# Pre-norm attention and FP8 linear layer on one core: transposed scores follow the plain ones at 16 steps in place of 32

## What is computed

```python
def reference(L0_attn_x, ...):                   # x: (16, 512, 256), fp32; 16 heads of 16
    ...
        qkv = jnp.einsum('bsd,ed->bse', x, qkv_w) + qkv_b
        ...
        scores = jnp.einsum('bhqe,bhke->bhqk', q, k) * scale
        attn = jax.nn.softmax(scores, axis=-1)
        out = jnp.einsum('bhqk,bhke->bhqe', attn, v)
        ...
        out = jnp.einsum('bsd,ed->bse', out, proj_w) + proj_b
    ...
        x_q = jnp.clip(x / input_scale, -FP8_MAX, FP8_MAX)
        x_dq = x_q.astype(jnp.float8_e4m3fn).astype(x.dtype) * input_scale
        out = jnp.einsum('bsi,oi->bso', x_dq, w_dq) + bias
    ...
    x = x + _L0_attn_ref(_layernorm(x, axis=-1), ...)
    x = x + _L0_ffn_ref(_layernorm(x, axis=-1), ...)
```

## Time and profile before

| what | value |
|---|---|
| three runs | 1053.39, 1055.44, 1057.67 us (median 1055.44) |
| profiled execution | 1050.12 us, span 1048.3 us |
| PE, DVE, ACT, POOL busy | 90%, 80%, 63%, 50% of the span |
| mean granted clock of TensorE | 0.954 |
| DMA | 79.4 MB, 50.5% of 16 engines |

### The profile page before, as it was taken

One profiled execution on the slowest core, in us unless ns is written; L12 is line 12 of the kernel. 1 busy time (PEld: TensorE's weight loads), 2 busy tenths in 40 slices (PEclk: granted clock), 3 DMA queues, 4 the chain that ended last, 5 costly groups with the idle time before them and its releaser, 6 DMA issues.

```text
span 1048.3 us, 16257 instructions
## 1 busy us (share of the span) xinstructions
PE 945.9 (90%) x5796; PEld 443.0 (42%) x5796; DVE 843.0 (80%) x1186; ACT 655.7 (63%) x1209; POOL 522.7 (50%) x533
## 2 busy tenths in 40 slices
PE   3476989999999999999999999999999999999884
PEld 2243334444444434454444444444444444433333
DVE  3586788888888989888888889888888888896226
ACT  3013776767676676767676676767676776766560
POOL 3141344828284654728293755638282846524242
PEclk9675999999999999999999999999999999999795
DMA  4928092656638192746648291836556380911010
GB/s 138 116 44 94 26 119 41 97 88 77 108 45 139 21 115 51 108 77 82 103 56 129 30 117 39 119 66 92 93 68 96 40 125 14 117 35 42 2 41 20
DMA packets 44289, 79.40 MB, mean 76 GB/s; under 512 B 9904, under 2 KB 13104, under 8 KB 44208
## 3 DMA queue, kind: packets, MB, share of 16 engines
q1 hardware_dynamic: 44208, 78.36, 50.5%
HBM read 18.42 MB, written 8.39 MB: 26 GB/s over the span
## 4 chain that ended last, share of the span: by engine, by line
PE 81%; ACT 6%; POOL 4%; DVE 3%; issue 2%; DMA 2%; SPq 1%; ACTq 0%; POOLq 0%; DVEq 0%
PE ps_t L457 28%; PE ps_o L489 23%; PE ps_m L371 9%; PE ps_s L471 5%; ACT pt L568 5%; PE ps_m L382 5%; PE ps_m L408 5%; PE ps_m L439 3%; POOL xnT_p L907 2%; SPq L282 1%; ACT xnT L587 1%; POOL xnT_p L905 1%; DVE mx L686 1%; DMA ks<-parts 1%; PE ps_m L355 1%
## 5 line engine op out<-in xcount | busy, mean ns | idle before, releaser
L568 ACT ACTIVATE pt<-ps_t 128x512 f32<-128x512 f32 x1024 | 557.5, 599 | 242.5 <-PE ps_t L457 238.0
L686 DVE TENSOR_REDUCE mx<-ps_s 128x2 f32<-128x1024 f32 x512 | 617.6, 1213 | 93.3 <-PE ps_s L471 87.9
L457 PE MATMUL ps_t<-qs,ks 50*128 50x512 f32 x1024 | 406.9, 467 | 41.1 <-ACT pt L568 34.7
L471 PE MATMUL ps_s<-ks,qs 48*128 48x512 f32 x1024 | 399.8, 472 | 20.0 <-DMA ks<-parts 11.4
L457 PEld LDWEIGHTS ps_t<-qs,ks 50*128 50x128 f32 x1024 | 164.7, 187 | 360.2 <-ACT pt L568 288.4
L489 PE MATMUL ps_o<-pt,vt 128*32 128x512 f32 x2048 | 275.3, 610 | 0.2 <-ACT pt L568 0.2
L471 PEld LDWEIGHTS ps_s<-ks,qs 48*128 48x128 f32 x1024 | 160.1, 189 | 31.3 <-DVE mx L686 16.1
L905 POOL CAST xnT_p<-xnT 128x512 fp32r<-128x512 f32 x30 | 18.3, 611 | 195.2 <-ACT xnT L587 195.2
L371 PE MATMUL ps_m<-xnT_p,wqkv_p 128*128 128x512 f32 x360 | 101.1, 417 | 7.6 <-POOL xnT_p L907 7.6
L939 POOL TENSOR_TENSOR on<-ot,rden 128x256 f32<-128x256 f32 x63 | 39.6, 628 | 103.8 <-DVE rden L745 103.8
L930 POOL TENSOR_TENSOR parts<-parts 128x512 f32<-128x512 f32 x60 | 81.2, 1353 | 4.9
(11 more groups left out here) (94 smaller groups left out, 766.4 us busy)
## 6 DMA issues: line engine op xcount, KB each, us to landing
qs<-parts SPq DMA_DIRECT2D x192, 128.0 KB, 6.5
ks<-parts SPq DMA_DIRECT2D x192, 128.0 KB, 7.0
xin<-in_x SPq DMA_DIRECT2D x16, 512.0 KB, 4.6
xres<-in_x SPq DMA_DIRECT2D x16, 512.0 KB, 5.9
out<-h SPq DMA_DIRECT2D x15, 512.0 KB, 9.0
qs<-nmax SPq DMA_DIRECT2D x128, 8.0 KB, 5.7
pt<-in_qkv_wT SPq DMA_DIRECT2D x1, 768.0 KB, 6.5
out<-h SPq DMA_DIRECT2D x2, 256.0 KB, 2.0
```

The lines of the kernel that those rows point to most:

```text
L457: nc.tensor.matmul(ps_t[:, g, :], ks[par][rows, slot, keys], qs[par][rows, slot, :], start=True, stop=True).then_inc(st_done, 1)
L471: done = nc.tensor.matmul(ps_s[:, s % 2, g, :], qs[par][rows, slot, queries], ks[par][rows, slot, :], start=True, stop=True)
L568: nc.scalar.activation(pt[n % 2][:, w % 2 + 2 * a, w // 2, :], ps_t[:, a, :], ACT.Exp, scale=SCALE).then_inc(exp_done, 1)
L686: dve.tensor_reduce(mx[:, t, :, s % (STEPS // 2)], ps_s[:, s % 2, :, :], AX_X, ALU.max).then_inc(max_done, 1)
```

## The change

The transposed scores of a batch now begin at step 16 of the slot that has its plain scores, and end at step 15 of the next one, not at steps 0 and 31 of the next one. For this the maxima go in four quarters of 8 steps: four transposes, four splits and 16 row transfers of 4 KB a batch where there were two, two and 8 of 8 KB. The stacks are sent in four groups of 6 transfers (q and k parts apart) where there were two of 12, and a batch's result in two halves. The heads of a quarter must be those whose plain scores are done, so the order of heads changes, with the rows of the projection weights. All steps of the side work are placed anew, and the orders on DVE, POOL and SP with them. The output projection is done in slot u = b + 2 and half of a batch's v projection in slot b.

```diff
-PROJECT_V = (4, 6)
-PROJECT_OUT = (8, 10)
-TRANSPOSE_X = (12, 14)
-PROJECT_QK = (16, 18, 20, 22)
-TRANSPOSE_MAX = (25, 5)
-TRANSPOSE_HQ = 26
-LINEAR = (28, 30)
-OUT_BLOCKS = (11, 19, 27, 3)
-OUT_BACK = (22, 5)
-COPY_OT = (24, 6)
...
+HALF_STEPS = STEPS // 2
+QUARTER = STEPS // 4
+NQ = 4
+
+PROJECT_V = (30, 0)
+TRANSPOSE_X = (2, 4)
+PROJECT_QK = (6, 12, 20, 22)
+TRANSPOSE_HQ = 10
+LINEAR = (14, 18)
+PROJECT_OUT = (26, 28)
+TRANSPOSE_MAX = (8, 16, 24, 1)
+OUT_BLOCKS = (27, 3, 11, 19)
+OUT_BACK = (6, 21)
+COPY_OT = (8, 23)
...
# SP, slot
             def slot(u, par, present):
                 if present(2):
-                    rows(u - 2, par, 1)
+                    rows(u - 2, par, 3)
                 if present(-2):
                     load(u + 2, par)
+                if present(1):
+                    rows(u - 1, 1 - par, 0)
                 if present(0):
                     stack(u, par, 0)
-                if present(1):
-                    rows(u - 1, 1 - par, 0)
                 if present(2):
                     reload(u - 2, par)
+                if present(3):
+                    store(u - 3, 0)
+                if present(1):
+                    rows(u - 1, 1 - par, 1)
                 if present(0):
                     stack(u, par, 1)
                 if present(3):
-                    store(u - 3, 1 - par)
+                    store(u - 3, 1)
+                if present(0):
+                    stack(u, par, 2)
+                if present(1):
+                    rows(u - 1, 1 - par, 2)
+                if present(0):
+                    stack(u, par, 3)
...
# PE, slot
                 for s in range(STEPS):
-                    if present(2):
-                        scores_t(u - 2, par, s, 0)
+                    bt, st = (u - 2, s + HALF_STEPS) if s < HALF_STEPS else (u - 1, s - HALF_STEPS)
+                    if 0 <= bt < B:
+                        scores_t(bt, bt % 2, st, 0)
...
# POOL, slot
             def slot(u, par, present):
-                later = not isinstance(u, int) or u > 0
-                if present(0):
-                    layernorm_x(u, par)
-                if present(3):
-                    out_divide(u - 3, 3)
-                    low_oT(u - 3, 1)
-                if present(0) and later:
+                if present(2):
+                    out_divide(u - 2, 1)
+                if present(0) and u > 0:
                     low_xnT(u, 0)
-                if present(2):
-                    out_divide(u - 2, 0)
-                if present(0) and later:
                     low_xnT(u, 1)
                 if present(3):
-                    layernorm_h(u - 3)
-                if present(0) and later:
+                    round_fp8(u - 3)
+                if present(0) and u > 0:
                     split(u, 0)
...
```

More of the change, by code:

```diff
@@ L156, in block_kernel @@
         stacked = [[sem(f"stacked{t}{i}") for i in range(2)] for t in range(NT)]
-        rows_in = [sem(f"rows_in{t}") for t in range(NT)]
-        stored = sem("stored")
+        rows_in = [sem(f"rows_in{r}") for r in range(NQ)]
+        stored = [sem(f"stored{i}") for i in range(2)]
         met = sem("met")
@@ L220, in present @@
             def present(u):
-                return lambda behind: 0 <= u - behind < B
+                return lambda behind, ends=B: 0 <= u - behind < ends
             for u in range(NSLOT - 1):
@@ L276, in stack, with rows @@
                 settled()
-                for r, (pq, pk) in enumerate(zip(Q_PARTS, K_PARTS)):
+                dst, picks = (qs, Q_PARTS) if n % 2 == 0 else (ks, K_PARTS)
+                for r, part in enumerate(picks):
                     for g in range(2):
                         rows = slice(HALF * g + HD * r, HALF * g + HD * (r + 1))
[L280 to L286, removed]
+                        sp.dma_start(dst[par][rows, NS * t:NS * (t + 1), :].bitcast(F32),
+                                     parts[HALF * g:HALF * (g + 1), n, part, :]).then_inc(stacked[t][par], 16)
+            def rows(b, par, r):
+                sp.wait_ge(nmax_split, 8 * b + 2 * r + 2)
                 settled()
@@ L358, in project_qk @@
             def project_qk(u, n):
-                start = isinstance(u, int) and u == 0
+                start = u == 0
                 bank = ps_s[:, n // 2, n % 2, :] if start else ps_m[:]
                 if not start:
-                    take_bank(u, "project_qk", n, 0)
+                    take_bank("project_qk", n, u)
                 if n == 0:
@@ L424, in transpose_hq, with linear @@
                 last.then_inc(xq_done, 1)
-            def linear(u, half, bank=None):
-                if isinstance(u, int) and u == 3:
+            def linear(b, half, bank=None):
+                if b == 0:
                     pe.wait_ge(const_v, 9)
                 if bank is None:
-                    take_bank(u, "linear", half, 3)
+                    take_bank("linear", half, b)
                     bank = ps_m[:]
                     if half == 0:
-                        pe.wait_ge(hqT_ready, u - 3 + 1)
+                        pe.wait_ge(hqT_ready, b + 1)
                 for j in range(2):
@@ L447, in scores_t @@
                 t, odd, kp = n // 4, n // 2 % 2, n % 2
-                slot = NS * t + 2 * (w % 2) + odd
-                if s in (0, STEPS // 2) and g == 0:
-                    pe.wait_ge(rows_in[t], 64 * b + 64)
-                    if isinstance(b, int) and b == 0:
+                slot = NS * t + 2 * odd + w % 2
+                if s % QUARTER == 0 and g == 0:
+                    pe.wait_ge(rows_in[s // QUARTER], 64 * b + 64)
+                    if b == 0:
                         pe.wait_ge(ks_ones, 16 * 16)
@@ L553, in finish @@
                     pe.wait_ge(hqT_ready, b + half + 1)
-                    linear(b + 3, half, ps_s[:, half, 1, :])
+                    linear(b, half, ps_s[:, half, 1, :])
             pe.wait_ge(ident_in, 32)
@@ L629, in slot @@
                         copy_hqT(u - 3)
+                    if s == PROJECT_V[0] and present(0):
+                        copy_v(u, par, 0)
             def finish(b):
@@ L1041 @@
     order = np.concatenate([order, np.arange(2 * D, 3 * D)])
+    place = np.arange(D).reshape(NT, 2, 2, 2, HD).transpose(0, 1, 3, 2, 4).reshape(-1)
     a = {k: np.asarray(v) for k, v in dict(
```

283 lines of the change are left out of this document (150 added, 133 removed).

## The result

The changed kernel takes **1092.96 us** (median of 4 runs, 1091.93 to 1098.74) against 1054.41 for the kernel before (1050.49 to 1057.67), a ratio of 1.040 with an interval of 1.037 to 1.043: slower by 38.6 us. The profiled execution took 1092.59 us, with a span of 1090.4; before it was 1050.12 and 1048.3, so the spans differ by 42.1. Of the runs further down, one execution of e1 (1233.28 us) and one of e4 (1405.49), each the profiled one, ran with TensorE's granted clock at 0.65 and 0.56 throughout, and their medians leave them out.

A forecast was written before the change was run, and what follows sets the result against it. A full slot was taken as bound by PE's order of work with small gaps. +6.3 + 1.4 + 29.9 - 1.0 - 20.9 = +15.7, with the clock +32.9, gave 1083.0, put at 1088 us on the median; range 1052 to 1109.

The forecast's parts named there:

- The start: Slot 1's beginning to slot 2's: 56.6 us in place of 50.3, +6.3 us, bounds +3 and +9.
- A full slot without new waits: Middle slots with the steps' new places: 57.63 us against 58.34, -0.7 us a slot.
- The chain: POOL's division ahead of both low parts delays step 6's scores 2.1 us, the q/k projection 3.0; +29.9 over slots 3 to 15.
- The clock: TensorE's gap ahead of the first q/k projection drops it to half rate: +1.23 us in 14 slots, +17.2.
- I take the projection alone: Only the first q/k projection runs at the low clock, 2.90 us for 1.67; upper bound adds half a low pair.
- The row the forecast leaned on: Profile row of q/k projections: 2.90 us at low clock, 1.67 at full, engine at full rate two projections on.
- Slot 2: Slot without hq and linear work: 59.7 us against 58.34, +1.4 us.
- Slot 16: No x work, so no new wait: 53.7 us against 54.74, -1.0 us.
- Slot 17: Last slot cut to 8 pairs and a linear layer, six pairs at low clock: 35.9 us, a gain of 20.9.
- SP: Queue issuing 16 transfers of maxima rows a batch, not 8: 4.9 us a slot more, hidden, zero cost.
- the tail's second linear layer: Batch 14's, now behind the last step: hidden by a wait for an exponential, else costs its own 1.1 us.
- Rival 3: POOL's order holds nobody up, full slots take 57.6 us: -26.3 us, 1029 us in all; chance 0.14.

The follow-up runs named there:

- e1: Changed kernel with POOL making the first low part of xn ahead of the division again, the second behind it; 1026.96 us, 0.972 of the kernel before.
- e4: Changed kernel, POOL's order kept, with the second half of the transposed xn in memory of its own (hq's); 1083.15 us, 1.024 of the kernel before.
- e6: e2 with DVE's two rounding-constant operations moved from steps 4 and 5 to step 1; 1025.90 us, 0.974 of the kernel before.
- e3: Changed kernel plus dummy matmuls, seven ahead of step 6's transposed scores and two ahead of the first q/k projection; 1062.60 us, 1.007 of the kernel before.
- e7: e1 with DVE's two rounding-constant operations moved from steps 4 and 5 to step 1; 1024.98 us, 0.973 of the kernel before.
- e2: Changed kernel with POOL's division placed behind both low parts of xn; 1032.61 us, 0.977 of the kernel before.
- e5: e1 plus dummy matmuls in slot 17's even steps, ahead of the last output projection and the transposes of hq; 1024.33 us, 0.972 of the kernel before.

## Why the prediction was right

It said 1088 us in a range of 1052 to 1109, and 1092.96 came out. In spans it forecast +32.9 us, and +42.1 came. By its steps:

- **The start**, +6.3 forecast. From slot 1's beginning to slot 2's it was 56.29 us against the 56.6 of the working. But slot 1 itself began at 37.09, not 39.77: 2.7 us that the forecast didn't have. Six transfers instead of twelve stand ahead of its first scores, which is the likely reason; no run tested it.
- **A full slot without new waits**, 57.6 forecast. e6 has 58.27 with a wait of 0.44, so 57.8.
- **The chain**, 3.0 us forecast: T+7.1 for the transposed score and T+8.75 for the projection, measured T+7.28 and T+8.90. The sum took 1.98 us for cast and subtraction of the first part, and beside L788 they took 2.28. The chain's cost by e3 and e6 is 3.1.
- **The clock**, 1.23 us a slot forecast, **mis-sized**: 2.2 measured by e3, as a mean. That it falls in every full slot was right; "I take the projection alone" held in part. The low stretches of slots 4, 5 and 11 in after:
```profile
232.00:235.40 3.40, 3.23 (x8) 2.23 (x10) 1.45 (x2) 0.46 (x2) 3.32 (x3) 0.50 0.00 0
293.40:300.20 6.80, 6.47 (x22) 2.83 (x20) 3.37 (x4) 2.97 (x5) 6.64 (x5) 0.50 0.00 0
672.30:689.40 17.10, 16.46 (x63) 6.36 (x63) 9.72 (x12) 8.07 (x15) 10.57 (x7) 0.50 0.19 32
```
In eight of slots 3 to 15 the clock was low for 3.4 us, little more than the projection, and the slot was 1.3 to 1.5 us longer than the same one in e3. In four it was low for 6.8 us, through step 7's values, which cost 2.4 to 2.7. In slot 11 it was low for 17.1 us, with TensorE busy for 16.46 of them, and that slot took 67.2 us, 6.3 more than in e3. What decides between these lengths no run shows. The row the forecast leaned on, told how soon the engine was fast again in another place. The Trainium skill ("TensorE: Matmul & The Clock Gate", HAM oscillation), which the prediction cited, has a rule of a loop throttled anew in every pass. It is borne out: in all 14 slots with this gap of 1.9 to 2.2 us the projection behind it took 2.21 to 2.90 us, against 1.67 at full clock.
- **Slot 2**, +1.4 forecast, was +3.6; it too pays the clock (61.95 against 59.65 in e3), which the sum had in another line. **Slot 16**, -1.0 forecast, was -1.1.
- **Slot 17**, -20.9 forecast, was -26.0: not six of its pairs were low but about three (25.4 + 3 x 1.75 = 30.7). e6 and e7 show that this number isn't the kernel's own: the stretch up to the last values differs by 4 us between them with no edit in slots 16 and 17 (by 8 between e2 and e7). A term like that wants a range and no count.
- **SP** was free: in the waits of after TensorE never waits for a DMA in slots 2 to 17, and the tail's second linear layer cost nothing that shows.

Per full slot -0.5, +3.1 and +2.2 make the +4.8 seen, where -0.7, +3.0 and +1.23 had been summed; the shorter start and slot 17 gave some 8 us of it back. The forecast also added 5 us because the median of before lay above its profiled execution, and after's did not (1092.96 against 1092.59). So that the total came within 5 us is in part luck: the span was 9 us off. Rival 3 had 1029 us for a kernel in which POOL's order holds nobody up. e1 is nearest to that kernel, and took 1026.96. That match is in part luck too, since a full slot took 58.57 and not 57.6, and other terms of the sum must have come out shorter to make up for it. What e1 and e3 do show is that the cause of the loss is the chain and the clock behind it, as forecast.

## What to carry to other kernels

When steps are moved, ask of each in-order queue not how long an operation takes there but how late its operand comes, and what stands behind it: a division of 0.62 us cost 4.6 us a slot, since it carried a reciprocal's lateness into the low part, ACT's copy, an exponential and a projection. A second buffer on the way doesn't help while the operand is late. And a gap on TensorE, here of 2 us, can cost itself and then the clock (the waits of 0.44 to 0.85 us in e5, e6 and e7 did not). The price varies from one pass to the next, so give it a range, or fill the gap, which here took the loss from 4.0% to 0.7% with work that computes nothing.

## What the hardware showed that was not expected

- DVE's L788 takes 0.67 us alone (e7) and 1.10 behind POOL's cast (e2); POOL's subtraction takes 1.60 behind it in place of 1.28, its division 1.12 behind L794 in place of 0.62 (e2 against e6). Both engines lose, where no semaphore joins them.
- The same gap in every slot of after was followed by a clock at 0.50 for 3.4, 6.8 or 17.1 us. In the longest TensorE was busy for 16.46 us of the 17.1, and the clock stayed low all the same.
- With the same matmuls in slot 17, whose pairs leave TensorE idle for 0.7 us each, e7 stayed at full clock, e6 ran 14 us at half and e2 24; the cause wasn't found. With two dummies a pair it stayed at full clock in all three versions that had them.
